# Inverse softmax sums spread over partitions by DMA instead of GpSimd, TensorE and ScalarE, with layer-norm rows in another instruction form and a split moved to GpSimd, in an attention and mixture-of-experts kernel

## What is computed

```python
h = layernorm(x) * (1 + ca) + sa
q, k, v = (h @ W.T for W in (Wq, Wk, Wv))            # 16 heads of 64
q = q / norm(q) * q_scale;  k = k / norm(k) * k_scale
attn = softmax(q @ k.T / 8)                           # per batch and head, 512 x 512
x = x + ga * (concat_heads(attn @ v) @ Wo.T + bo)
h = layernorm(x) * (1 + cb) + sb
x = x + gb * moe(h)    # router, top 2 of 8 experts with a capacity, shared expert
```

## Time and profile before

| | |
|---|---|
| time, median of 3 runs | 1409.95 us (1408.2 to 1410.84) |
| the profiled execution: its own time | 1406.78 us |
| its span in the profile | 1405.0 us |
| PE busy | 1262.1 us, 90% of the span |
| DVE busy | 1107.3 us, 79% |
| ACT busy | 952.9 us, 68% |
| POOL busy | 858.0 us, 61% |
| mean granted TensorE clock | 0.959 of full speed |

### The profile page before, as it was taken

One profiled execution on the slowest core, in us unless ns is written; L12 is line 12 of the kernel. 1 busy time (PEld: TensorE's weight loads), 2 busy tenths in 40 slices (PEclk: granted clock), 3 DMA queues, 4 the chain that ended last, 5 costly groups with the idle time before them and its releaser, 6 DMA issues. The chain is left out here.

```text
span 1405.0 us, 31811 instructions
## 1 busy us (share of the span) xinstructions
PE 1262.1 (90%) x9674; PEld 828.6 (59%) x9674; DVE 1107.3 (79%) x1995; ACT 952.9 (68%) x2014; POOL 858.0 (61%) x1659
## 2 busy tenths in 40 slices
PE   4899999989999999999899999999994477899997
PEld 4555565656555565556566555666552355677775
DVE  3778878878878887788788788877873996788887
ACT  3677677767666776677677766777762565777776
POOL 2577666766666776666667667676754664444443
PEclk8899999999999999999999999999998699999999
DMA  5000000000000000000000000000002000535341
GB/s 131 2 2 1 2 1 2 2 4 2 1 4 2 2 2 4 2 2 2 4 1 2 3 2 2 2 1 2 2 1 75 1 0 9 131 86 104 89 89 38
DMA packets 53202, 28.60 MB, mean 20 GB/s; under 512 B 8720, under 2 KB 51224, under 8 KB 53016
## 3 DMA queue, kind: packets, MB, share of 16 engines
q1 hardware_dynamic: 51832, 25.99, 7.7%
q10 hardware_dynamic: 1184, 0.40, 0.1%
HBM read 24.16 MB, written 2.23 MB: 19 GB/s over the span
## 5 line engine op out<-in xcount | busy, mean ns | idle before, releaser
L697 ACT ACTIVATE probs<-bank,neg_max 128x512 f32<-128x512 f32 x512 | 347.5, 684 | 280.3 <-DVE neg_max L815 259.5
L815 DVE TENSOR_REDUCE neg_max<-bank 128x1 f32<-128x512 f32 x512 | 329.3, 685 | 165.4 <-PE bank L516 162.0
L556 PE MATMUL bank<-probsT,qkv 128*64 128x512 f32 x1024 | 280.7, 628 | 0.9 <-DVE oT L832 0.9
L516 PE MATMUL bank<-operands 64*128 64x512 f32 x1536 | 255.9, 439 | 0.9 <-DVE operands L810 0.5
L993 POOL TENSOR_TENSOR inv_wide<-inv_sum,consts 128x512 f32<-128x512 f32 x64 | 66.5, 1039 | 237.7 <-DVE inv_sum L826 237.7
L532 PEld LDWEIGHTS T<-ident,probs 64*128 64x128 f32 x4096 | 173.6, 142 | 40.3 <-issue 10.2
L532 PE MATMUL T<-ident,probs 64*128 64x64 f32 x4096 | 173.6, 226 | 1.5 <-issue 0.7
L486 PEld LDWEIGHTS bank<-operands,hT_h 128*128 128x128 f32 x254 | 48.2, 190 | 213.0 <-issue 209.4
L516 PEld LDWEIGHTS bank<-operands 64*128 64x128 f32 x1536 | 128.4, 190 | 63.5 <-issue 44.2
L1627 POOL TENSOR_TENSOR hid_l<-gated,hid_h 128x512 fp32r<-128x512 f32 x64 | 89.4, 1397 | 123.3 <-ACT hid_h L1544 123.3
L977 POOL TENSOR_TENSOR sq<-qkv 128x256 f32<-128x256 f32 x252 | 150.9, 615 | 11.9 <-ACT qkv L676 9.7
(11 more groups left out here) (235 smaller groups left out, 2399.7 us busy)
## 6 DMA issues: line engine op xcount, KB each, us to landing
probsT<-gate_scratch SPq DMA_DIRECT2D x64, 256.0 KB, 4.9
out<-x_all SPq DMA_DIRECT2D x8, 256.0 KB, 2.3
probsT<-in_L_ffn_fc_w SPq DMA_DIRECT2D x1, 1024.0 KB, 9.4
raw<-in_L_attn_Wq SPq DMA_DIRECT2D x1, 512.0 KB, 4.4
raw<-in_L_attn_Wk SPq DMA_DIRECT2D x1, 512.0 KB, 7.3
raw<-in_L_attn_Wv SPq DMA_DIRECT2D x1, 512.0 KB, 8.6
raw_o<-in_L_attn_Wo SPq DMA_DIRECT2D x1, 512.0 KB, 8.7
probsT<-in_L_ffn_sh_w SPq DMA_DIRECT2D x2, 256.0 KB, 2.7
```

Of the source, the lines that this page charges most:

```text
L516: last = nc.tensor.matmul(s_bank(hp, 2 * pair + head)[:], own[rows, q, toks], own[rows, k], start=((q, k) == (QH, KH)), stop=(q == QL))
L556: last = nc.tensor.matmul(O_BANK[rows, :], qkv[:, hp % 4, j, cols], probsT[:, hp % 2, head, j], start=(j == 0), stop=(j == NT - 1), skip_g ...
L697: nc.scalar.activation(probs[:, i % 4], s_bank(hp, i)[:], ACT.Exp, bias=neg_max[:, i:i + 1], accum_out=row_sum[:, hp % 2, i:i + 1]).then_i ...
L815: nc.vector.reduce_max(neg_max[:, i:i + 1], s_bank(hp, i)[:], AX.X, negate=True).then_inc(max_done, 1)
```

## The change

The inverse sums no longer pass through POOL, PE and ACT. SP writes them (128 x 8 single values) to a buffer in memory, waits until they are there, and reads them back twice, once for each head of the pair, each read copying rows of 512 bytes to 64 partitions. It does so for each unit, in a loop over the batches like the other engines'. widen, inverse_rows and copy_inverse are gone, and normalise waits for the reads. ln_rows uses scalar_tensor_tensor with the inverse deviation as a broadcast second tensor. split_h1 moves from DVE to POOL: all four tiles at the end of slot 5, and for batch 0 ahead of everything else; its high part is a multiplication by one.

```diff
-                    last = nc.vector.tensor_scalar(h_ln[:, t], tile_of(b, t), mean_var[:, t, 0:1], rstd[:, t:t + 1],
-                                                   ALU.subtract, ALU.mult)
+                    last = nc.vector.scalar_tensor_tensor(out=h_ln[:, t], in0=tile_of(b, t), scalar=mean_var[:, t, 0:1],
+                                                          in1=rstd[:, t:t + 1].to_broadcast([P, C]), op0=ALU.subtract,
+                                                          op1=ALU.mult)
...
+            inv_scratch = nc.dram_tensor("inv_scratch", [2, S_TILES, P], F32).ap()
...
+                    def spread_inverse(w, hp):
+
+                        sp.wait_ge(inv_done, w + 1)
+                        sp.dma_start(inv_scratch[hp % 2].rearrange("k q -> q k"), inv_sum[:, hp % 2]).then_inc(inv_out, 16)
+                        sp.wait_ge(inv_out, 16 * (w + 1))
+                        for head in range(2):
+                            sp.dma_start(inv_row[head * DH:(head + 1) * DH, hp % 2].rearrange("p (t q) -> p t q", t=NT),
+                                         inv_scratch[hp % 2].rearrange("(t h) q -> h t q", h=2)[head].partition_broadcast(DH)
+                                         ).then_inc(inv_in, 16)
...
                             if main and pair == 0:
                                 side = between(b, hp, u)
-                            if pair == 1 and earlier >= 1:
-                                inverse_rows(u - 1, side)
-                                side = (r_copied, u)
                             if main and pair == 2 and with_next(b, hp, 1):
                                 transpose_q(u + 1, hp + 1, side)
...
                     def normalise(u, hp):
                         dve.wait_ge(av_step, NT * (u + 1))
-                        dve.wait_ge(r_copied, u + 1)
+                        dve.wait_ge(inv_in, 32 * (u + 1))
...
+                    def split_h1(b, t):
+                        pool.wait_ge(h1_done, b + 1)
+                        after(pool, pj_ready, NT * (HP * b - 1) + t + 1)
+                        toks = slice(t * P, (t + 1) * P)
+                        nc.gpsimd.tensor_tensor(hT_h[:, toks], h1_out[:, toks], c1.to_broadcast([P, P]), ALU.mult).then_inc(h1h_done, 1)
+                        pool.wait_ge(h1h_done, NT * b + t + 1)
+                        nc.gpsimd.tensor_tensor(hT_l[:, toks], h1_out[:, toks], hT_h[:, toks].bitcast(F32),
+                                                ALU.subtract).then_inc(hT_ready, 1)
...
-                        if earlier >= 1:
-                            widen(u - 1, hp - 1)
                         if main and with_next(b, hp, 1):
                             normalise_qk(u + 1, hp + 1)
...
+                        if main and hp == HP - 3 and not is_const(b, LAST):
+                            for t in range(NT):
+                                split_h1(b + 1, t)
```

More of the change, by code:

```diff
@@ L364, in adaln_attention_moe @@
             inv_sum = sb("inv_sum", [P, 2, S_TILES])
-            inv_wide = sb("inv_wide", [P, NT, 2, DH])
             inv_row = sb("inv_row", [P, 2, N])
             oT = sb("oT", [P, N])
+            inv_scratch = nc.dram_tensor("inv_scratch", [2, S_TILES, P], F32).ap()
             oT_h = sb("oT_h", [P, HP, N], F32R)
@@ L400, in adaln_attention_moe @@
             inv_done = sem("inv_done")
-            wide_done = sem("wide_done")
-            r_ready = sem("r_ready")
-            r_copied = sem("r_copied")
+            inv_out = sem("inv_out")
+            inv_in = sem("inv_in")
             av_step = sem("av_step")
@@ L467, in _, with batch @@
                 def _(sp):
+                    def spread_inverse(w, hp):
[6 more added lines that the diff above has]
+                                         ).then_inc(inv_in, 16)
+                    def batch(b):
+                        for hp in range(HP):
+                            if not (is_const(b, 0) and hp == 0):
+                                spread_inverse(HP * b + hp - 1, hp - 1)
+                    over_batches(sp, batch)
+                    spread_inverse(HP * B - 1, HP - 1)
                     sp.wait_ge(av_step, NT * HP * B)
@@ L535, in transpose_probs @@
                         last.then_inc(t_ready, 1)
-                    def inverse_rows(u, *free):
-                        pe.wait_ge(wide_done, u + 1)
-                        for semaphore, value in free:
-                            after(pe, semaphore, value)
-                        for t in range(NT):
-                            last = nc.tensor.transpose(XT_BANK[:, t * P:(t + 1) * P],
-                                                       inv_wide[:, t].rearrange("p h d -> p (h d)"), ident[:])
-                        last.then_inc(r_ready, 1)
                     def weigh_values(u, hp, j):
@@ L664, in _ @@
                         weigh_values(HP * B - 1, HP - 1, j)
-                    project_out(LAST, 3, (r_copied, HP * B), (y_more, 3 * LAST + 2))
+                    project_out(LAST, 3, (y_more, 3 * LAST + 2))
                     transpose_y(LAST)
@@ L702, in copy_transposed @@
                         nc.scalar.activation(pair_tiles(hp, pair), t_pair, ACT.Copy).then_inc(t_act, 1)
-                    def copy_inverse(u, hp):
-                        act.wait_ge(r_ready, u + 1)
-                        after(act, o_done, u - 1)
-                        nc.scalar.activation(inv_row[:, hp % 2], XT_BANK[:], ACT.Copy).then_inc(r_copied, 1)
                     def modulate1(b):
@@ L744, in slot @@
                                     modulate2(b - 1)
-                            if pair == 1 and earlier >= 1:
-                                copy_inverse(u - 1, hp - 1)
                             if main and pair == 2 and with_next(b, hp, 1):
@@ L824, in invert_sums @@
                         dve.wait_ge(p_done, S_TILES * (u + 1))
-                        after(dve, wide_done, u - 1)
+                        after(dve, inv_out, 16 * (u - 1))
                         nc.vector.reciprocal(inv_sum[:, hp % 2], row_sum[:, hp % 2]).then_inc(inv_done, 1)
@@ L897, in norm_first @@
                             ln_rows(dve, *rows)
-                        if not is_const(b, LAST) and (hp, pair) in ((5, 1), (5, 2), (5, 3), (6, 0)):
-                            split_h1(b + 1, (pair - 1) % NT)
                     def norm_last(b, hp, pair):
@@ L946, in _ @@
                     take_mod(mod1, (CA, SA), 0, mod1_done, (h1_done, 0))
-                    for t in range(NT):
-                        split_h1(0, t)
                     sum_squares(0)
@@ L987, in normalise_qk @@
                             nc.gpsimd.tensor_tensor(rows, rows, by, ALU.mult).then_inc(qn_done, 1)
-                    def widen(u, hp):
-                        pool.wait_ge(inv_done, u + 1)
-                        after(pool, r_ready, u)
-                        src = inv_sum[:, hp % 2].rearrange("p (t h) -> p t h", h=2)
-                        nc.gpsimd.tensor_tensor(inv_wide[:], src.unsqueeze(3).to_broadcast([P, NT, 2, DH]),
-                                                c1.unsqueeze(2).unsqueeze(3).to_broadcast([P, NT, 2, DH]),
-                                                ALU.mult).then_inc(wide_done, 1)
+                    def split_h1(b, t):
[6 more added lines that the diff above has]
+                                                ALU.subtract).then_inc(hT_ready, 1)
                     def split_o(u, hp):
@@ L1025, in batch @@
                             slot(b, hp)
+                    for t in range(NT):
+                        split_h1(0, t)
                     normalise_qk(0, 0)
```

8 lines of the change are left out of this document (removed).

## The result

| | median us | runs | ratio to before, 95% |
|---|---|---|---|
| before, beside it | 1410.39 | 1408.2 to 1413.79 | |
| changed kernel | 1429.03 | 1422.5 to 1450.87 | 1.0115 [1.0081, 1.0149] |

The changed kernel is 1.15% slower; 1375.4 us was forecast, and the range ended at 1392. Its profiled execution (1450.87 us) was a disturbed one, with a granted clock of 0.94 and longer than the others (1422.5 to 1429.77); single instructions and waits are read from it here, not its sum.

A forecast was written before the change was run, and what follows sets the result against it. PE was taken to bound ordinary slots, by small margins. Terms 29.7 + 2.4 + 3.5 + 2.2 - 0.5 - 3.4 + 0.7 = 34.6 us saved gave 1375.4 us against the median 1409.95; range 1352 to 1392.

The forecast's parts named there:

- The DMAs: Write and two reads of each unit's inverse sums: about 6 us, at most about 20, under 23.6, so no cost.
- The rival in which the chain is late in every slot: DMA chain from sums to use exceeds its time; 25 us would add 57, to about 1432 us; chance 0.04.
- The end of the attention: Last unit's sums to their use, without slack: 0.7 us saved; a chain of 20 us loses 11.
- a chain of 6: DMA write and reads taking 6 us at the last unit, which would give all 1.7 us saved.
- Transposes on PE: Removing the inverse-sum transposes before the scores in pair 1 saves 0.53 us in 56 slots, 29.7 us.
- slot 3: L39's guess no longer meets POOL's long multiplication: 0.5 us in 7 batches, 3.5 saved, bounds 0 and 6.6.
- The rival that it is not passed on: ACT or DVE end last once PE loses its 0.53 us: 1405 if all lost, 1390 if half; chance 0.10.
- widen: Removed from POOL: transpose_q's wait of some 0.4 us goes in six slots, 2.4 us saved.
- Splits: Moved from DVE to POOL: slot 5's row maxima 0.34 us earlier, about 2.2 saved; 0.5 lost in batch 0.
- Layer norm: ln_rows' new form still takes turns with POOL: 0.06 us more each, 3.4 lost over 14 layer norms.
- the first rival: ln_rows' new form escapes POOL, four rows taking about 1.2 us instead of 3.07: 1327 us; chance 0.08.
- Low clock: Stretches of slowed PE clock, one more or less in each batch: 1.7 x 7 = 12 us in the range.

The follow-up runs named there:

- the first experiment: Four kernels testing whether the DMAs cost the time; its first, the changed kernel without DMAs and with inv_row set to ones, saved 34.1 us.
- e1: Changed kernel without its DMAs, inv_row set to ones once; 34.1 us faster than the kernel before.
- e3: Changed kernel with the write sent as 128 rows of 32 bytes instead of 1024 values of 4 bytes, same reads; 1379.5 us.
- e4: Changed kernel with widen, inverse_rows and copy_inverse back and no DMA, leaving the layer norm's form and the splits; 0.26% slower than the kernel before.
- e6: Changed kernel with the table of inverse sums transposed on TensorE, copied by ScalarE and written as 8 rows of 512 bytes; 1388.5 us.

## Why the prediction was wrong

**The step that failed is "The DMAs": "Both are under 23.6: no cost."** Two things in it were wrong, and only the smaller is a size. The write was sized at 2.4 us by projT, the nearest by the count of its values; it takes 9.7 to 11. But the text's own bound for the chain, 20 us, covers even that, and the rows were indeed never late in a slot. The larger fault is that a DMA was taken to cost only by being late. This one costs 50 us (1429.0 - 1379.5), and only the 15.28 - 7.80 = 7.5 at the end of the attention are for being late. Beside the kernel before, where nobody waits for it, it costs 44.7: while it is under way VectorE and ScalarE stand still, up to 6.1 us at a time. The rival in which the chain is late in every slot named the same line and the same direction (1432), but its mechanism did not take place, so that its number comes close is an accident.

Why do the engines stand still? Shown is that it needs the writes of neighbouring single values (a gap of 4 bytes removes it), that no engine of the core releases the waits, and that every long one begins while a write is under way. The changed kernel has 51 waits for "remote" of 1 us or more. None begins sooner than 4.7 us behind the issue of a write, and they end between 2.6 us before and 0.9 us behind the moment at which SP goes on; 16 of them end within 0.3 us of it, like the two shown. The packets that bring instructions become slower as well: 16 KB on q8 take 1.06 us in the kernel before and 1.86 in the changed one, 8 KB on q14 0.42 and 0.98.

My theory before the first experiment was that instruction loads are held up and the engines stand still for want of them. The trace speaks against it as the whole cause: in 27 of the 51 waits no packet of q8 or q14 is under way, the 5.10 us above among them, and with eight writes, where these packets are slowest (2.76 and 2.12 us), there is no wait for "remote" at all. What the engines wait for stays open. The run with half of the values has only six such waits, 9.9 us together, and still lost 29 us; so part of the loss lies in short delays that the view of the waits does not name. Why neighbouring 4-byte writes are slow to land is open too; 8 bytes of room for each are enough (3.9 us), and 512 pairs of 8 bytes side by side do no harm either (3.3).

**The end of the attention** was taken as 0.7 saved. It lost 15.28 - 9.21 = 6.1 us, inside the bound of 11 that the text gave for a slow chain. With the write as 128 rows it saves 9.21 - 7.80 = 1.4, near the 1.7 of a chain of 6.

**The other terms held as a sum, in part by luck.** Without the DMAs' cost it is 34.1 us (e1) or 33.5 (e3) between medians, where 34.6 was forecast, the end included. Between the two profiled executions, from which the slots below are read, it is 1405.0 - 1377.1 = 27.9: that of the kernel before had a granted clock of 0.959, while its executions beside e1 to e4 had 0.951 to 0.956. The transposes brought 56 x 0.44 = 24.6 of their 29.7, and slot 3 (5.1 instead of 3.5) and the end (1.4 instead of 0.7) made up for 2.3 of the missing 5.1. Mean lengths of a slot in batches 1 to 6, from first scores to first scores (the changed kernel's is the execution of 1450.87 us):

```
slot              0      1      2      3      4      5      6      7
before          16.93  16.88  14.35  17.60  15.88  15.66  15.36  16.91
e3_rows32       16.82  15.95  13.91  16.79  15.32  14.92  14.92  17.57
changed kernel  18.24  16.15  14.64  17.48  15.76  16.39  17.63  19.96
```

*Transposes on PE*: 0.44 a slot and not 0.53, since the projection and the scores do not close up fully (0.72 from one to the other, where 0.63 was left by the earlier trace rows); slots 2 and 6 show it pure. The rival that it is not passed on fell. *widen*: slots 2 to 4 of batch 0 went from 14.57 to 14.59 us down to 13.77 or 13.78, 0.8 with the transposes' 0.44, so 0.35 for the wait of the earlier trace rows; 0.4 was said. *Slot 3* gained 0.80 in all, 0.5 was said. Its mechanism held: without widen the guess at L39 takes 0.17 us instead of 0.94, and in the kernel that has widen back (e4) 0.96. *Splits*: slot 5 gained 0.74, of which 0.30 is theirs; 0.34 was said. The first scores of all came 0.33 us later (38.05 to 38.38; 38.63 in the changed kernel); 0.5 was said.

*Layer norm*: locked out as before, a little longer in slot 0, as forecast. Timeline of slot 0 of batch 3 in the changed kernel, the counterpart of the earlier trace rows:

```profile
445.49 3.48 DVE L200 SCALAR_TENSOR_TENSOR h_ln<-x_all,mean_var,rstd 128x128 f32<-128x128 f32 x4
...
446.31 1.27 POOL L987 TENSOR_TENSOR oT_l<-oT,oT_h 128x512 fp32r<-128x512 f32 x1
...
450.91 0.63 PE L593 MATMUL bank<-ident,h_ln 128*128 128x128 f32 x4 [2.54 <-DVE operands L808]
```

3.48 against 3.07, and PE waits 2.54 against 2.17: 0.4 for the four, where 0.24 was said. In slot 3, for which the prediction also took 3.07, it was 3.39 before and is 3.36 with 128 rows; nothing is lost there. Where the waiting has moved the rows away from GpSimd's long instructions, as in slot 0 of batch 4 of the changed kernel, four of them take

```profile
584.90 1.13 DVE L200 SCALAR_TENSOR_TENSOR h_ln<-x_all,mean_var,rstd 128x128 f32<-128x128 f32 x4
```

and the old form took 1.11 with GpSimd idle, at 14.32 us of the kernel before. So neither form is slow by itself, both wait for GpSimd, and the first rival (the new form escapes GpSimd, 1327 us) fell. The rule of the Trainium skill, "SBUF — State Buffer", section "SBUF: two separate sides", that a VectorE instruction with two SBUF inputs asks for the shared ports as well, agrees with these rows; "VectorE: DVE Perf Modes", section "Mode 2×_2P — use both read ports for one tensor", taken alone pointed the other way, and these rows show no such gain. The kernel with both small parts alone (e4) was 0.26% slower than before, 3.7 us, where their terms sum to 1.7 lost (3.4 and 0.5 lost, 2.2 gained): the sign was right.

*Low clock*: slot 7 became longer, by 0.66 us in the mean, and unevenly: 18.5, 18.7, 18.6, 16.9 and 17.8 us in batches 1 to 5 of e3, against 17.2 in each before. At the end of a batch, where the loop jumps back, PE is idle for nothing that the profile shows ("issue"). This hole was 1.84 to 1.94 us before, and the clock stayed at 1.00 behind all five. It is 1.96 to 2.44 in e3, and behind four of five the clock fell; behind that of batch 3 (2.16 us) it did so as follows. Windows of both kernels over that stretch (length, busy of PE, PEld, DVE, ACT, POOL, then PEclk); first the one with 128 rows, then the kernel before:

```profile
530.00:534.00 4.00, 3.59 (x9) 2.69 (x9) 1.80 (x5) 0.49 (x1) 1.59 (x8) 0.57 0.05 9
```

```profile
548.00:552.00 4.00, 3.80 (x33) 2.82 (x35) 3.24 (x8) 0.49 (x1) 1.65 (x4) 1.00 0.03 8
```

The same matmuls of 128x512 took 0.63 instead of 0.39 us each. The prediction's range spoke of such stretches, one more or less in each batch (1.7 x 7). They came here and went elsewhere: slot 1 of batches 1 and 6 takes 14.92 and 14.95 us in e3, where it took 16.9. That the longer hole lowers the clock is not shown: in the kernel with the turn on TensorE (e6) it fell behind holes of 1.85 to 1.88 us too.

## What to carry to other kernels

Ask of a transfer not only whether it lands in time but what its shape does meanwhile: a write to memory whose 4-byte values come from different partitions and end up side by side made VectorE and ScalarE stand still here, and the others behind them, even where nobody waited for it. Turn such a table on the chip first (a TensorE transpose, a 32x32 turn on VectorE, or a DMA within SBUF), and write whole rows; here this makes 1429 into 1388, and the loss of 1% into a gain of 1.7%. And where a trace shows engines idle for something "remote", with their inputs ready, look for a write that was issued and has not landed; the packets of the DMA queues alone do not show it, since here they were over long before.

## What was not expected of the hardware

- 128 neighbouring single values take 6.7 us to land in memory, 512 take 8.3 and 1024 take 9.7; with 8 bytes from value to value 1024 take 3.9, with 64 bytes 2.4. 1024 transfers of 32 bytes, eight times the bytes, take 2.1. These are means of SP's waits beyond the issue. The packets of 1024 single values are through 1.59 us behind the issue whether they land early or late.
- 128 rows of 32 bytes take 1.3 us, 8 rows of 512 bytes 0.9 (54.9 us in 64 waits).
- The transpose of a 128x8 table and ScalarE's copy of 8x128, 0.27 and 0.25 us by themselves, lengthen an ordinary slot by 0.11 us (slot 6: 15.03 in e6 against 14.92 in e3), where the four transposes had cost 0.44.
- With the same instructions the clock behind the loop's jump can be 0.57 in one batch and 1.00 in the next (e3, batches 3 and 4); what decides is not shown.
